# Relative-attention kernel: a semaphore for each buffer of relative products, and the stores of probabilities issued by ScalarE instead of SyncE

## The reference, cut to what matters

```
xn = _layernorm(x);  q, k, v = proj(xn)                     # 16 heads of 8
idx  = clip(pos_k - pos_q, -20, 20) + 20
attn = softmax((einsum('bhqd,bhkd->bhqk', q, k) + einsum('bhqd,qkd->bhqk', q, rel_k[idx])) / sqrt(8))
w    = einsum('bhqk,bhkd->bhqd', attn, v) + einsum('bhqk,qkd->bhqd', attn, rel_v[idx])
out  = w @ Wo.T + bo
```

## Time and profile before

| | us |
|---|---|
| median of 3 runs (2433.53 to 2444.78) | 2439.86 |
| the profiled execution, its own time | 2443.62 |
| its span, first to last instruction | 2441.8 |
| PE busy in it | 2122.4 |
| DVE busy | 1852.5 |
| ACT busy | 1594.5 |
| POOL busy | 1030.8 |

### The profile page before, as it was taken

The page is one execution under the profiler, slowest core; times in us unless marked ns, Lnnn a source line. Parts: engine busy times, 40 slices in busy tenths (PEclk is TensorE's granted clock), DMA queues, the critical chain, the costliest instruction groups (busy, mean ns, idle before and its releaser), DMA issues. The chain is left out here.

```text
span 2441.8 us, 77225 instructions
## 1 busy us (share of the span) xinstructions
PE 2122.4 (87%) x27816; PEld 1453.6 (60%) x27816; DVE 1852.5 (76%) x4151; ACT 1594.5 (65%) x4178; POOL 1030.8 (42%) x1270
## 2 busy tenths in 40 slices
PE   3389888889888888889888888599999978999999
PEld 1266666566666666666666666356656645666665
DVE  1388889789889879879889889266776746777777
ACT  2388788788788878788788778267777743223222
POOL 4246556656656656655655644100000003333331
PEclk7699999999999999999999999699999989999999
DMA  3355655655655555555655653101001020110100
GB/s 100 106 123 130 148 133 127 152 134 128 150 142 127 148 141 123 145 141 123 148 141 120 146 116 78 43 14 35 30 26 38 27 70 18 34 30 26 34 30 18
DMA packets 571232, 228.63 MB, mean 94 GB/s; under 512 B 465590, under 2 KB 543030, under 8 KB 566326
## 3 DMA queue, kind: packets, MB, share of 16 engines
q1 hardware_dynamic: 570934, 224.63, 37.1%
HBM read 129.61 MB, written 94.90 MB: 92 GB/s over the span
## 5 line engine op out<-in xcount | busy, mean ns | idle before, releaser
L821 ACT ACTIVATE a_probs<-a_bank_s,a_neg_max 128x512 f32<-128x512 f32 x1024 | 697.3, 691 | 149.0 <-DVE a_neg_max L682 139.1
L483 PE MATMUL a_bank_pt<-a_ident,a_probs 128*128 128x128 f32 x4096 | 597.3, 286 | 103.5 <-ACT a_qr L741 49.0
L682 DVE TENSOR_REDUCE a_neg_max<-a_bank_s 128x2 f32<-128x1024 f32 x512 | 627.0, 1225 | 55.4 <-DVE a_bank_s L647 0.9
L483 PEld LDWEIGHTS a_bank_pt<-a_ident,a_probs 128*128 128x128 f32 x4096 | 449.3, 144 | 237.1 <-issue 94.4
L664 DVE COPY a_probs_t<-a_bank_pt 128x512 f32<-128x512 f32 x512 | 350.2, 684 | 78.2 <-PE a_bank_pt L483 72.6
L795 ACT ACTIVATE a_probs_t<-a_bank_pt 128x512 f32<-128x512 f32 x512 | 310.4, 606 | 83.3 <-PE a_bank_pt L483 81.2
L505 PE MATMUL a_bank_o<-a_probs_t,a_v 128*32 128x128 f32 x8192 | 286.9, 282 | 1.8 <-DVE a_probs_t L664 0.3
L1544 ACT ACTIVATE e_gate<-e_bank_g 128x512 f32<-128x512 f32 x144 | 85.9, 597 | 274.2 <-PE e_bank_g L1483 274.2
L505 PEld LDWEIGHTS a_bank_o<-a_probs_t,a_v 128*32 128x32 f32 x8192 | 215.5, 112 | 58.1 <-issue 49.4
L943 POOL TENSOR_TENSOR a_win<-a_raw,a_band 128x1152 f32<-128x1152 f32 x64 | 168.8, 2638 | 176.5 <-issue 92.0
L647 DVE TENSOR_TENSOR a_bank_s<-a_bank_s,a_win 128x144 f32<-128x144 f32 (+2 forms) x640 | 161.3, 271 | 106.1 <-PE a_bank_s L471 102.8
(11 more groups left out here) (167 smaller groups left out, 3555.9 us busy)
## 6 DMA issues: line engine op xcount, KB each, us to landing
scr_probs<-a_probs SPq DMA_DIRECT2D x512, 72.0 KB, 2.6
a_raw<-scr_qr SPq DMA_DIRECT2D x256, 96.0 KB, 2.5
scr_qr<-a_qr SPq DMA_DIRECT2D x64, 320.0 KB, 4.0
a_feat<-scr_probs SPq DMA_DIRECT2D x256, 78.0 KB, 2.5
scr_parts<-a_sp SPq DMA_DIRECT2D x144, 128.0 KB, 2.5
a_left<-scr_probs SPq DMA_DIRECT2D x256, 64.0 KB, 2.4
a_q<-scr_parts SPq DMA_DIRECT2D x32, 192.0 KB
a_k<-scr_parts SPq DMA_DIRECT2D x32, 192.0 KB
```

What stands on the lines that cost most here:

```text
L483: ins = nc.tensor.transpose(b_pt[bank_of(job)][:, 0, t * P:(t + 1) * P], probs[(u - 1) % 4][:, j, MAX_REL + t * P:MAX_REL + (t + 1) * P], ...
L682: nc.vector.tensor_reduce(neg_max[:, 2 * pair:2 * pair + 2], b_s[:, 2 * pair:2 * pair + 2, :], AX.X, ALU.max, negate=True).then_inc(max_ok, 1)
L821: nc.scalar.activation(probs[u % 4][:, j, MAX_REL:MAX_REL + S], b_s[:, j, :], ACT.Exp, bias=neg_max[:, j:j + 1], accum_out=sums[:, t, PLAC ...
```

## The change

The change has two parts. `out_qr` becomes a list of two semaphores, one for each buffer `QR[0]` and `QR[1]`. A store signals that of its buffer, `read_qr` waits for `16 * (t // 2)` on that of its own buffer on top of `8 * NT` for each row before, and SyncE's two waits for all stores of a row become two waits each, with one `sem_inc(room, 1)` after each wait in the loop.

The two stores of probabilities of each unit, 32 a row, go from SyncE's stream to ScalarE's. The new function `store(b, u - 1)` stands in ScalarE's unit `u` between the second block copy and the exponentials of pair 1. The waits for `f_in` and `l_in` at the first unit of a quarter and the wait for `exp_ok` move with it; the latter is then for exponentials that ScalarE itself computed one unit earlier. The transfers have the same shape, addresses and semaphores.

```diff
-        out_xn, out_sp, out_qr, out_0 = sem("out_xn"), sem("out_sp"), sem("out_qr"), sem("out_0")
+        out_xn, out_sp, out_0 = sem("out_xn"), sem("out_sp"), sem("out_0")
+        out_qr = [sem(f"out_qr{k}") for k in range(2)]
...
-                sp.dma_start(scr["qr"][n * NT + t], QR[t % 2][:].rearrange("p h r -> p (h r)")).then_inc(out_qr, 16)
+                sp.dma_start(scr["qr"][n * NT + t], QR[t % 2][:].rearrange("p h r -> p (h r)")).then_inc(out_qr[t % 2], 16)
...
                         if t == 1 and not last:
-                            sp.wait_ge(out_qr, 16 * NT * (b + 2))
+                            for k in range(2):
+                                sp.wait_ge(out_qr[k], 8 * NT * (b + 2))
+                                sp.sem_inc(room, 1)
...
-                    if tail:
-                        continue
-                    if u % 4 == 0:
-                        need(sp, f_in, b, 64 * NT, 64 * (t - 1))
-                        need(sp, l_in, b, 64 * NT, 64 * (t - 1))
-                        sp.sem_inc(room, 1)
-                    sp.wait_ge(exp_ok, b * 4 * UNITS + 4 * u + 4)
-                    for i in (0, 2):
-                        at = PROBS_AT[t % 2] + (i * H + head_of(u, i) * NJ) * QBLK * WIN
-                        own = probs[u % 4][:, PLACES.index(i), t * P + i * QBLK:]
-                        sp.dma_start(bass.AP(scr["probs"].tensor, at, [[WIN, P], [H * QBLK * WIN, 2], [1, WIN]]),
...
-            sp.wait_ge(out_qr, 16 * NT)
+            for k in range(2):
+                sp.wait_ge(out_qr[k], 8 * NT)
...
-                    need(act, out_qr, n, 16 * NT, 16 * 2 * (t // 2))
+                    need(act, out_qr[t % 2], n, 8 * NT, 16 * (t // 2))
...
+            def store(b, u):
+
+                t = u // 4
+                if u % 4 == 0:
+                    need(act, f_in, b, 64 * NT, 64 * (t - 1))
+                    need(act, l_in, b, 64 * NT, 64 * (t - 1))
+                act.wait_ge(exp_ok, b * 4 * UNITS + 4 * u + 4)
+                for i in (0, 2):
+                    at = PROBS_AT[t % 2] + (i * H + head_of(u, i) * NJ) * QBLK * WIN
+                    own = probs[u % 4][:, PLACES.index(i), t * P + i * QBLK:]
+                    act.dma_start(bass.AP(scr["probs"].tensor, at, [[WIN, P], [H * QBLK * WIN, 2], [1, WIN]]),
+                                 bass.AP(own.tensor, own.offset,
+                                         [own.ap[0], [2 * (S + 2 * MAX_REL) + QBLK, 2], [1, WIN]])
+                                 ).then_inc(p_out[u % 4], 16)
...
                         if (u and not tail) or (u == 0 and not first):
                             read_probs(b, u, 2 * pair)
+                        if pair and u:
+                            if not tail:
+                                store(b, u - 1)
+                        elif pair and not first:
+                            store(b - 1, UNITS - 1)
```

More of the change, by code:

```diff
@@ L382, in row @@
                         sp.dma_start(scr["y"][b - 1], y_in[:]).then_inc(y_st, 16)
-                    if tail:
-                        continue
-                    if u % 4 == 0:
-                        need(sp, f_in, b, 64 * NT, 64 * (t - 1))
-                        need(sp, l_in, b, 64 * NT, 64 * (t - 1))
-                        sp.sem_inc(room, 1)
-                    sp.wait_ge(exp_ok, b * 4 * UNITS + 4 * u + 4)
-                    for i in (0, 2):
-                        at = PROBS_AT[t % 2] + (i * H + head_of(u, i) * NJ) * QBLK * WIN
-                        own = probs[u % 4][:, PLACES.index(i), t * P + i * QBLK:]
-                        sp.dma_start(bass.AP(scr["probs"].tensor, at, [[WIN, P], [H * QBLK * WIN, 2], [1, WIN]]),
-                                     bass.AP(own.tensor, own.offset,
-                                             [own.ap[0], [2 * (S + 2 * MAX_REL) + QBLK, 2], [1, WIN]])
-                                     ).then_inc(p_out[u % 4], 16)
             for sm, start in ((y_st, 16), (y_ok, 2)):
```

## The result

The changed kernel takes 2423.19 us (median of 9 runs, 2415.04 to 2428.35), the kernel before 2439.86 in the same comparison: a ratio of 0.9935, interval 0.9916 to 0.9953. It is 16 us faster, where 40 were forecast. The profiled execution has a span of 2413.3 us against 2441.8. It is at the fast end of its runs and the one before is above its median, so the 28 us between the two spans overstate the gain.

A forecast was written before the change was run, and what follows sets the result against it. No engine alone was taken to set the pace: ScalarE, VectorE and TensorE, 81 to 87% busy, wait for each other. With 61 us off and 21 on, 40 us faster: 2400 us, forecast's range 2368 to 2427, 8-in-10 range 2368 to 2490.

The forecast's parts named there:

- The 14 long waits go: ScalarE's waits before `read_qr`, one in each of rows 0 to 13, 45.0 us together, all vanish; worth 61 us.
- the straight line: Fit of thirteen full batch rows' lengths against their long waits: slope 1.36, 86.2 us a row at no wait.
- They go because of the semaphores: Before `read_qr` in unit 14, ScalarE would wait only for quarter 0's store, issued 4.9 us before quarter 1's.
- the ordinary coupling: ScalarE's short waits for the maximum, 137.4 us, and a transposed block, 79.8 us; pieces of at most 2.4 us.
- The first rival: Gain given back: all 64 us of store lateness passed on, 2443 us; or wait misread, 2461 us; chance 0.15.
- is worth nothing directly: Taking 32 store issues a row off SyncE: compute engines wait for no load there, only 3.4 us for a store.
- The price of the stores: Issues before pair 1's exponentials on ScalarE: 0.25 us late a unit, 64 us, a third reaching the end: 21 us.
- second rival: ScalarE's arithmetic waits for the issues in full: rows of 96.5 us, 96 us on, 2536 us; chance 0.10.
- third rival: SyncE's and ScalarE's issues delay each other: a pair takes 1.64 us, 102 us on less 61, 2481 us; chance 0.17.

The follow-up runs named there:

- Part one alone: Kernel before with only the two semaphores, stores left on SyncE: 2431.51 us against 2430.41, ratio 1.0006.
- earlier place: Changed kernel with ScalarE's two store issues ahead of the second block copy, behind the exponentials of pair 0: 2376.66 us, ratio 0.9776 to the kernel before.
- behind pair 1: Changed kernel with ScalarE's two store issues moved behind the exponentials of pair 1 of the same unit: 2372.40 us, ratio 0.9744 to the kernel before.
- the version with the large loads: Kernel before with two semaphores, stores on SyncE, 18 loads of q and k a row issued by ScalarE ahead of the second copy: 2518.85 us, ratio 1.0342.
- four issues a unit: Changed kernel with each store cut into two of half the size, all issued by ScalarE: 2707.27 us, ratio 1.1136 to the kernel before.

## Why the prediction was wrong

The direction was right, and the measured time lies in the range. The size isn't: 16 us of gain instead of 40. By its own steps:

- **The 14 long waits go, and that is worth 61 us**: right for the change as a whole. Where ScalarE pays nothing, the gain is 0.0224 to 0.0260 of 2430, 54 to 63 us. The batch rows there take 85.6 to 86.1 us, nearly all at clock 1.00, where the straight line came to 86.2 at no wait.
- **They go because of the semaphores** ("all 14 waits to be gone" by part one, "what is late next at that place is the ordinary coupling"): wrong. Part one alone brings nothing (ratio 1.0006). The first rival had that outcome only for the case that the wait was for something else; it was for the store of quarter 1, since it went when that store got its own semaphore, and still nothing was won. Late next was the landing of the stores of probabilities, issued by the same late queue. The step that failed is the one that took SyncE to be on time: the prediction has the store of unit u issued "at about the end of u", and in the trace before it starts 6.2 us after that end in the mean, more than a unit, and 12.2 us in unit 13. The earlier trace rows had a sign of it, two such waits with 3.4 us. The prediction said that the stores' removal from SyncE "is worth nothing directly"; it was the part that earned the gain. That the sum holds 61 us all the same is luck: both parts were in the change, and the other one earned them.
- **The price of the stores, 21 us**: the term that spoiled the size. The mechanism was as described: the issues begin with the copy, and the exponentials of pair 1 come late. The lateness is 1.04 - 0.66 = 0.38 us a unit, where I took 0.25, 97 us over 256 units instead of 64. I had read the room off one unit, in which the exponentials begin 0.85 us after the copy; in the mean it is 0.66. Of the lateness 39 to 46 us reach the end, 40 to 47%, where I took a third. The change ended about halfway between the forecast and the first rival, but by neither's sizes: the rival had all of 64 us passed on, and it was less than half of 97.
- **The sum with measured terms**: 54 to 62 us off (earlier place, behind pair 1), 39 to 46 on, which leaves 16. The price is the difference between those versions and the change, so this splits the 16 us and doesn't check them.
- **Smaller slips**: the row that the earlier trace rows shows as the longest, 93.5 us, isn't; the one from 833.1 to 927.1 takes 94.0, with a wait of 4.10 us, so a row's length isn't set by this wait alone. The slope of 1.36 was taken over all thirteen and stands. The lower end of the forecast's range comes to 2369 by its own terms, and the upper one, 2427, isn't worked out from any.
- **ScalarE stops while it issues** (second rival): refuted. Exponentials run on during an issue, to the hundredth, in the version with the earlier place.
- **The two streams get into each other's way** (third rival): not in the change, where a store on ScalarE's queue takes 421 ns in the median and 480 in the mean, less than the 465 and 546 on SyncE's before, and a pair takes 1.00 us instead of the rival's 1.64. In the version with the large loads it did happen, but to SyncE. There two issues of ScalarE, of 0.28 and 0.72 us, begin and end within a single one of SyncE's, which runs from 608.55 for 5.39 us. So an issue isn't shut out for the whole recorded length of the other's. The Trainium skill ("Perfetto Trace Analysis", section "DMA Instruction — HWDGE (DVE, Sync)") says that the block is locked for one at a time, but also that the recorded length of an issue includes the wait for this lock. The trace doesn't contradict it, then, and doesn't show where in the 5.39 us the lock was held.

## What to carry to other kernels

A long wait behind a queue that runs late can be a symptom: here, with its semaphore split, the next wait on the same queue paid the same time. Ask what that queue issues last before each of its waiters, and relieve it. An issue moved to a computing engine cost next to nothing here while older instructions of that engine still ran, and was felt where it outlasted them, so put it behind the longest work whose waits are already met, or where the engine waits anyway, and not in front of the operand that is always ready.

## What the runs showed of the hardware

- An issue of half the bytes took as long as a whole one: 453 ns in the median for 36 KB on ScalarE's queue (four issues a unit), 421 ns for 72 KB (the change).
- An issue on ScalarE's queue doesn't wait for the end of the instruction ahead of it. With the earlier place it starts 0.012 us in the median after the start of the arithmetic instruction before it, which has 0.6 us or so to run. Where the next exponential is held up by the issues (the change, four issues), it starts 0.125 us in the median after their end.
- Two queues at once, one with loads of up to 192 KB: a single issue of `feat` on the other took up to 8.4 us, against 2.1 in the kernel before, where the longest issue of the attention, a store of 320 KB, took 4.2. The mean of all of SyncE's issues in the attention rose from 0.59 to 0.68 us.
